# One subtraction (kt_l) moved from GpSimd to VectorE in a gated-linear-attention and channel-mix layer

## The chip, the cores and the metric

The kernel runs on all 8 cores of one Trainium2 chip. Each core works alone on its own slice of the tokens. The metric is the device time in microseconds (us) of the slowest core. The engines of a core are called here PE (TensorE), DVE (VectorE), ACT (ScalarE), POOL (GpSimd) and SP (SyncE, which issues all DMAs).

## The reference

The layer has two halves, each added back to its input through a layer norm. All sizes are fixed: 2 sequences of 16384 tokens, width 1024, 8 heads of 128.

```python
# first half: gated linear attention on x = layernorm(input)
q = silu(x @ Wq.T)
f = sigmoid(x @ Wk.T)
log_f = log_sigmoid(f)
k = 1.0 - f
v = x @ Wv.T
# per head, over time:  S = exp(g_t)[:, None] * S + k_t[:, None] * v_t[None, :];  o_t = q_t @ S
out = rmsnorm(gla_scan(q, k, v, log_f), norm_w) @ Wo.T
x = input + layernorm(out)
# second half: channel mix on layernorm(x), with the token before mixed in
xr = mu_r * x + (1 - mu_r) * x_prev;  xk = mu_k * x + (1 - mu_k) * x_prev
out = sigmoid(xr @ W_r.T) * (square(relu(xk @ W_k.T)) @ W_v.T)
x = x + layernorm(out)
```

## The kernel before, in words

Each core gets 4096 tokens and 256 warm-up tokens ahead of them, so 4352 tokens or 17 tiles of 256 (`TILE`). Data lies transposed: the 1024 features are 8 blocks of 128 partitions, the tokens run along the free dimension. Every float32 operand X of a matmul is split in two bfloat16 tensors, X_h = bf16(X) and X_l = bf16(X - X_h), and each product is made of three matmuls (h*h, h*l, l*h).

Phase A (attention) runs first over all tiles, then phase B (output projection and channel mix), with its own weights. The change lies in phase A alone.

Phase A treats a tile as two chunks of 128 tokens (`cc` 0 and 1). The loop has 18 rounds for 17 tiles: in round `it` it prepares the projections of tile p = it and works through the attention of tile q = it - 1. The order in which the parts of a round are written is: `a_bc(p)`, `a_prep(2q)`, `a_prep(2q+1)`, `a_vproj(2q)`, `a_gla(2q)`, `a_vproj(2q+1)`, `a_ln(p)`, `a_wk(p)`, `a_gla(2q+1)`, `a_wq(p)`, `a_stats(p+1)`. Each engine executes its own instructions in exactly this order; between engines there are only counting semaphores, one per engine (V for DVE, S for ACT, G for POOL, T for PE), and an instruction waits at the head of its queue until the counts it names are reached.

`a_prep` builds the operands of one chunk. Its instructions, in order:

- DVE L329: 8 running sums (one per head) of the log gate, `b_sb`. The first waits for the 8 exponentials of the chunk before (`ebx_done`), which read the old `b_sb`.
- ACT L333: `ebq` = exp(b + 44). ACT L336: `ebk` = exp(-b - 44).
- DVE L339: `qt_scr` = q * ebq. DVE L343: `qt_h`, the bfloat16 copy. DVE L345: `qt_l` = qt_scr - qt_h.
- POOL L349: `ebk` = k * ebk. ACT L353: `kt_h`, the bfloat16 copy. POOL L356: `kt_l` = ebk - kt_h. This last one is what the change moves.
- ACT L361: 8 exponentials (one per head) into `ebq`. POOL L367: `ebq` = k * ebq. ACT L370: `kx_h`. POOL L373: `kx_l`.

`a_vproj` has 48 matmuls of 512 columns on PE (L400) and then four DVE instructions that take the two PSUM banks out as `vt_h` (L408, L410) and `vt_l` (L412, L415). `a_gla` has 24 matmuls kt x qt into two PSUM banks (L446, these read `kt_h` and `kt_l`), their masking and splitting on DVE (L457, L460, L462, once per bank), 24 matmuls of the cross-chunk part (L479, which overwrite the same banks and so wait for L462), its splitting on DVE (L491, L494), and the output matmuls (L514, L531), which ACT takes out of PSUM (L547, L552). `a_ln` has four DVE instructions on 128 x 2048, `a_wk` and `a_wq` have 192 matmuls each (L250), `a_stats` has the row sums for the layer norm (L231, L235) and small DVE and ACT work on one partition.

`kt_h`, `kt_l`, `qt_h`, `qt_l` have two buffers (`par`), so both chunks of a tile are prepared before the first is used. `ebk` and `ebq` have one.

Of the kernel before, what the change touches and what calls it, by code (L numbers as in the profile page):

```python
# [24 lines left out]
class Bld:  # L25
# [12 lines left out]
    def op(self, eng, fn, wait=(), inc=(), nop=False):  # L38
        wmax = {}
        for s, v in wait:  # L40
            if v > 0:
                wmax[s] = max(v, wmax.get(s, 0))
        waits = tuple((self.sem[s], v) for s, v in wmax.items())
        ev = None
        incs = []
        for s, k in inc:
            self.cnt[s] += k
            incs.append((self.sem[s], k))
            ev = (s, self.cnt[s])

        def closure(e, fn=fn, waits=waits, incs=tuple(incs), nop=nop):
            for sem, v in waits:
                e.wait_ge(sem, v)
            if nop:
                e.engine_nop()
            ins = fn(e)
            for sem, k in incs:
                ins.then_inc(sem, k)

        self.q[eng].append(closure)  # L60
        return ev
# [27 lines left out]
    def ev(self, s):  # L89
        return (s, self.cnt[s])  # L90


def build_program(tok, warm, debug=False):
# [31 lines left out]
    op, ev, C = bld.op, bld.ev, bld.cnt  # L125
# [30 lines left out]
    for dst, src in ((mask4, mask4v), (onesc, onescv), (onesr, onesrv),  # L156
                     (nw, nwv), (mur, murv), (muk, mukv)):
        op("sync", lambda e, dst=dst, src=src: e.dma_start(out=dst[:], in_=src),
           inc=[("LW", 16)])
# [111 lines left out]
    ebk = ctxA.enter_context(nc.sbuf_tensor("ebk", [128, H, CH], F32))  # L271
    qt_h = ctxA.enter_context(nc.sbuf_tensor("qt_h", [128, 2, H, CH], BF16))
    qt_l = ctxA.enter_context(nc.sbuf_tensor("qt_l", [128, 2, H, CH], BF16))
    kt_h = ctxA.enter_context(nc.sbuf_tensor("kt_h", [128, 2, H, CH], BF16))
    kt_l = ctxA.enter_context(nc.sbuf_tensor("kt_l", [128, 2, H, CH], BF16))
# [44 lines left out]
    def a_prep(gc):  # L320
        q, cc = gc // 2, gc % 2
        tsl = slice(cc * CH, (cc + 1) * CH)
        par = gc % 2
        tpar = gc % 3
        fpar = q % 2
        aq = at[q]
        for h in range(H):
            wv = [aq["ev_g"], ("V", C["V"]), st["ebx_done"]] if h == 0 else ()
            op("vector", lambda e, h=h, tsl=tsl: e.tensor_tensor_scan(  # L329
                b_sb[:, h, :], g_sb[:, h, tsl], g_sb[:, h, tsl], 0.0, ALU.add, ALU.bypass),  # L330
               wait=wv, inc=[("V", 1)], nop=True)
        ev_b = ev("V")
        ev_ebq = op("scalar", lambda e: e.activation(out=ebq[:], in_=b_sb[:], func=AF.Exp,  # L333
                                                     bias=b_p44[:, 0:1]),
                    wait=[ev_b, st["ebq_free"], ("S", C["S"])], inc=[("S", 1)])
        ev_ebk = op("scalar", lambda e: e.activation(out=ebk[:], in_=b_sb[:], func=AF.Exp,  # L336
                                                     bias=b_m44[:, 0:1], scale=-1.0),
                    wait=[ev_b, st["ebk_free"]], inc=[("S", 1)])
        op("vector", lambda e, tsl=tsl, fpar=fpar: e.tensor_tensor(  # L339
            qt_scr[:], fq_sb[:, fpar, :, tsl], ebq[:], ALU.mult),  # L340
           wait=[aq["ev_q"], ev_ebq, ("V", C["V"])], inc=[("V", 1)])
        ev_qtmul = ev("V")
        op("vector", lambda e, par=par: e.tensor_copy(qt_h[:, par], qt_scr[:]),  # L343
           wait=[st["qt_free"][par], ("V", C["V"])], inc=[("V", 1)])
        op("vector", lambda e, par=par: e.tensor_tensor(qt_l[:, par], qt_scr[:],  # L345
                                                        qt_h[:, par], ALU.subtract),
           wait=[("V", C["V"])], inc=[("V", 1)])
        ev_qt = ev("V")
        op("gpsimd", lambda e, tsl=tsl: e.tensor_tensor(ebk[:], k_sb[:, :, tsl], ebk[:],  # L349
                                                        ALU.mult),  # L350
           wait=[aq["ev_k"], ev_ebk, ("G", C["G"])], inc=[("G", 1)])
        ev_ktmul = ev("G")
        ev_kth = op("scalar", lambda e, par=par: e.activation(  # L353
            out=kt_h[:, par], in_=ebk[:], func=AF.Copy),
            wait=[st["kt_free"][par], ev_ktmul, ("S", C["S"])], inc=[("S", 1)])
        op("gpsimd", lambda e, par=par: e.tensor_tensor(kt_l[:, par], ebk[:], kt_h[:, par],  # L356
                                                        ALU.subtract),
           wait=[ev_kth, ("G", C["G"])], inc=[("G", 1)])
        ev_kt = ev("G")
        for h in range(H):  # L360
            op("scalar", lambda e, h=h: e.activation(  # L361
                out=ebq[:, h, :], in_=b_sb[:, h, :], func=AF.Exp, scale=-1.0,
                bias=b_sb[:, h, CH - 1:CH]),
               wait=[ev_qtmul, ev_b, ("S", C["S"])], inc=[("S", 1)])
        ev_ebx = ev("S")
        st["ebx_done"] = ev_ebx
        ev_kxmul = op("gpsimd", lambda e, tsl=tsl: e.tensor_tensor(  # L367
            ebq[:], k_sb[:, :, tsl], ebq[:], ALU.mult),
           wait=[ev_ebx, ("G", C["G"])], inc=[("G", 1)])
        ev_kxh = op("scalar", lambda e, tpar=tpar: e.activation(  # L370
            out=kx_h[:, tpar], in_=ebq[:], func=AF.Copy),
            wait=[st["kx_free"][tpar], ev_kxmul, ("S", C["S"])], inc=[("S", 1)])
        op("gpsimd", lambda e, tpar=tpar: e.tensor_tensor(kx_l[:, tpar], ebq[:],  # L373
                                                          kx_h[:, tpar], ALU.subtract),
           wait=[ev_kxh, ("G", C["G"])], inc=[("G", 1)])
        ev_kx = ev("G")
        st["kx_ready"][tpar] = ev_kx
        st["ebq_free"] = ev_kx
        st["ebk_free"] = ev_kt
        st["k_free"] = ("G", C["G"])  # L380
        if cc == 1:
            st["fq_free"][fpar] = ev_qtmul
            st["g_free"] = ev_b
        prep.setdefault(gc, {}).update(
            dict(ev_b=ev_b, ev_qt=ev_qt, ev_kt=ev_kt, par=par, tpar=tpar))
# [271 lines left out]
    for it in range(nt + 1):  # L657
        p, q = it, it - 1
        if p < nt:
            a_bc(p)  # L660
        if q >= 0:
            a_prep(2 * q)
            a_prep(2 * q + 1)
            a_vproj(2 * q)
            a_gla(2 * q)
            a_vproj(2 * q + 1)
        if p < nt:
            a_ln(p)
            a_wk(p)
        if q >= 0:  # L670
            a_gla(2 * q + 1)
        if p < nt:
            a_wq(p)
            if p + 1 < nt:
                a_stats(p + 1)
        bld.flush()
# [355 lines left out]
```

How the kernel before makes its waits and increments, by code:

```python
        def closure(e, fn=fn, waits=waits, incs=tuple(incs), nop=nop):  # L51
            for sem, v in waits:
                e.wait_ge(sem, v)
            if nop:
                e.engine_nop()
            ins = fn(e)
            for sem, k in incs:
                ins.then_inc(sem, k)
# [11 lines left out]
        def closure(e, waits=waits):  # L70
            for sem, v in waits:
                e.wait_ge(sem, v)
```

## Time and profile before

| | |
|---|---|
| median of 2 runs | 5805.86 us (5741.52 and 5870.21) |
| profiled execution, its own time | 5803.8 us |
| profiled execution, span of the slowest core (5) | 5801.9 us |
| profiled execution, fastest core (2) | 5730.5 us |
| phase A, rounds with attention | about 245 to 2650 us of the span, 17 rounds |
| phase B, tiles | from about 2868 us to the end |

The profile is of one execution, and its page is of core 5, the slowest. "Busy" is the time in which an engine executes; "idle before" an instruction is put down to what released it, as inferred from the semaphores. The "granted clock" is the share of full speed that TensorE was granted in a stretch. All eight cores do the same work on different tokens.

### The profile page before, as it was taken

To read this page: it belongs to the slowest core of one execution; us is meant where nothing else is said; L and a number is where in the kernel's file an instruction comes from. 1 tells how busy PE (TensorE), PEld (TensorE's weight loads), DVE (VectorE), ACT (ScalarE), POOL (GpSimd) and SP (SyncE) were. 2 spreads that over 40 slices of the span, in tenths; PEclk is the share of its full clock that TensorE was granted. 3 is DMA by queue.
4 is the path that set the end of the run, shared out by engine and by line. 5 is a ranking of instruction groups with operands and counts; after the bars stand their busy time and mean duration, and the time that the engine had idled before them with its cause. 6 is when DMAs were issued, how large, how long until landed. Compare 5 with 4: busy or idle time off the path is not lost.

```text
span 5801.9 us, 65888 instructions; the slowest of 8 cores (5730.5 to 5801.9 us)
## 1 busy us (share of the span) xinstructions
PE 3535.2 (61%) x26608; PEld 2641.5 (46%) x26608; DVE 1951.1 (34%) x1944; ACT 1059.1 (18%) x1597; POOL 530.6 (9%) x239
## 2 busy tenths in 40 slices
PE   0566666666666666661166556766565667665676
PEld 0344444444444444441155444555444455544454
DVE  1333333333333333342133333232333332233323
ACT  0222222222222222230011111111111111111010
POOL 1111111111111111111200000000000000000000
PEclk9877778777777777775588778888887877777777
DMA  2000000000000000002200000000000000000000
GB/s 81 26 15 14 15 15 15 14 15 15 15 15 15 15 15 15 15 8 62 76 15 15 22 22 22 22 1 23 22 22 22 22 22 1 22 22 22 22 8 8
DMA packets 114735, 121.83 MB, mean 21 GB/s; under 512 B 3683, under 2 KB 107270, under 8 KB 114438
## 3 DMA queue, kind: packets, MB, share of 16 engines
q1 hardware_dynamic: 114438, 117.63, 6.6%
q8 instruction: 215, 3.52, 0.3%
q14 instruction: 82, 0.67, 0.0%
HBM read 83.00 MB, written 34.62 MB: 20 GB/s over the span
## 4 chain that ended last, share of the span: by engine, by line
PE 53%; DVE 26%; ACT 7%; DMA 5%; issue 5%; POOL 3%; DVEq 1%; ACTq 0%; SPq 0%; POOLq 0%
PE p_pj L250 39%; PE p_st L231 4%; PE p_pj L400 3%; DVE b_sb L329 3%; PE p_O L514 1%; PE p_O L531 1%; DVE r_a L207 1%; DMA outT<-x_sb 1%; ACT ebq L361 1%; DVE p_A L457 1%; DVE qt_h L343 1%; PE p_A L479 1%; DVE A_l L462 1%; DVE A_h L460 1%; DMA oB<-o_scr 1%
## 5 line engine op out<-in xcount | busy, mean ns | idle before, releaser
L250 PE MATMUL p_pj<-o_pair,woh 128*128 128x256 bf16 x2176 | 423.5, 302 | 538.1 <-POOL o_pair L763 306.1
L250 PEld LDWEIGHTS p_pj<-o_pair,woh 128*128 128x128 bf16 x2176 | 232.0, 108 | 599.5 <-issue 553.4
L231 PE MATMUL p_st<-x_sb,onesc 128*1 128x256 f32 x544 | 182.3, 509 | 475.1 <-ACT oB L897 270.6
L250 PE MATMUL p_pj<-ln_h,wkh 128*128 128x256 bf16 x1088 | 308.3, 283 | 199.6 <-DVE ln_l L613 199.6
L250 PE MATMUL p_pj<-xk_h,wv2h 128*128 128x256 bf16 x1088 | 318.6, 293 | 118.9 <-DVE xk_l L821 118.9
L231 PEld LDWEIGHTS p_st<-x_sb,onesc 128*1 128x1 f32 x544 | 55.3, 105 | 601.1 <-issue 577.6
L250 PE MATMUL p_pj<-o_pair,wol 128*128 128x256 bf16 x1088 | 327.0, 301 | 0.0
L250 PE MATMUL p_pj<-xr_h,wrh 128*128 128x256 bf16 x1088 | 306.5, 282 | 24.8 <-DVE xk_l L938 24.8
L250 PE MATMUL p_pj<-xk_l,wv2h 128*128 128x256 bf16 x1088 | 318.4, 293 | 0.0
L250 PE MATMUL p_pj<-xk_h,wv2l 128*128 128x256 bf16 x1088 | 317.5, 292 | 0.0
L250 PE MATMUL p_pj<-ln_h,wqh 128*128 128x256 bf16 x1088 | 310.7, 286 | 2.5 <-ACT fq_sb L648 2.5
L250 PE MATMUL p_pj<-ln_h,wql 128*128 128x256 bf16 x1088 | 309.9, 285 | 0.0
L250 PE MATMUL p_pj<-ln_l,wqh 128*128 128x256 bf16 x1088 | 309.6, 285 | 0.0
L250 PE MATMUL p_pj<-ln_l,wkh 128*128 128x256 bf16 x1088 | 308.5, 284 | 0.0
L250 PE MATMUL p_pj<-ln_h,wkl 128*128 128x256 bf16 x1088 | 307.3, 282 | 0.0
L250 PE MATMUL p_pj<-xr_h,wrl 128*128 128x256 bf16 x1088 | 306.4, 282 | 0.0
L250 PE MATMUL p_pj<-xr_l,wrh 128*128 128x256 bf16 x1088 | 306.3, 282 | 0.0
L250 PE MATMUL p_pj<-xk_h,wk2h 128*128 128x256 bf16 x1088 | 303.2, 279 | 0.0
L250 PE MATMUL p_pj<-xk_l,wk2h 128*128 128x256 bf16 x1088 | 303.2, 279 | 0.0
L250 PE MATMUL p_pj<-xk_h,wk2l 128*128 128x256 bf16 x1088 | 303.2, 279 | 0.0
L479 PE MATMUL p_A<-qt_h,kx_h 128*128 128x128 bf16 x264 | 71.4, 280 | 370.9 <-DVE A_l L462 370.9
L761 POOL CAST o_pair<-oB 128x2048 bf16<-128x2048 f32 x17 | 32.1, 1889 | 2524.4 <-DMA oB<-o_scr 2524.4
(176 smaller groups left out, 7956.9 us busy)
## 6 DMA issues: line engine op xcount, KB each, us to landing
x_sb<-xT SPq DMA_DIRECT2D x17, 1024.0 KB, 5.4
o_scr<-o_stage SPq DMA_DIRECT2D x68, 256.0 KB, 2.3
oB<-o_scr SPq DMA_DIRECT2D x17, 1024.0 KB, 5.4
xB<-xT SPq DMA_DIRECT2D x17, 1024.0 KB, 5.5
outT<-x_sb SPq DMA_DIRECT2D x16, 1024.0 KB, 4.5
wstage<-wkT SPq DMA_DIRECT2D x8, 512.0 KB
wstage<-wqT SPq DMA_DIRECT2D x8, 512.0 KB
wstage<-wvT SPq DMA_DIRECT2D x8, 512.0 KB
```

The costliest lines, as they stand in the source:

```text
L207: op("vector", lambda e: e.reciprocal(r_a[:], r_t0[:]), wait=[("S", C["S"])], inc=[("V", 1)], nop=True)
L231: op("tensor", lambda e, ci=ci: e.matmul(p_st[0:1, 0:TILE], onesc[:], x_ap[:, ci, :], start=(ci == 0), stop=(ci == NCH - 1)), wait=wv if c ...
L250: e.matmul(bank[:, 0:TILE], wop[:, ci, dj * 128:(dj + 1) * 128], xop[:, ci, :], start=first, stop=last),
L329: op("vector", lambda e, h=h, tsl=tsl: e.tensor_tensor_scan(b_sb[:, h, :], g_sb[:, h, tsl], g_sb[:, h, tsl], 0.0, ALU.add, ALU.bypass), wa ...
L343: op("vector", lambda e, par=par: e.tensor_copy(qt_h[:, par], qt_scr[:]), wait=[st["qt_free"][par], ("V", C["V"])], inc=[("V", 1)])
L361: op("scalar", lambda e, h=h: e.activation(out=ebq[:, h, :], in_=b_sb[:, h, :], func=AF.Exp, scale=-1.0, bias=b_sb[:, h, CH - 1:CH]), wait ...
L400: e.matmul(bank[:], lnop[:, ci, tsl], wop[:, ci, half * 512:(half + 1) * 512], start=first, stop=last),
L457: op("vector", lambda e, bank=bank: e.tensor_tensor(bank[:], bank[:], mask4[:], ALU.mult), wait=[ev_Amm[g4], ("V", C["V"])], inc=[("V", 1)])
L460: op("vector", lambda e, bank=bank, Ah=Ah: e.tensor_copy(Ah[:], bank[:]), wait=[("V", C["V"])], inc=[("V", 1)])
L462: op("vector", lambda e, bank=bank, Ah=Ah, Al=Al: e.tensor_tensor(Al[:], bank[:], Ah[:], ALU.subtract), wait=[("V", C["V"])], inc=[("V", 1)])
L479: e.matmul(bank[:, (h - 4 * g4) * 128:(h - 4 * g4 + 1) * 128], kop[:, xpar, h, :], qop[:, h, :], start=first, stop=last),
L514: e.matmul(obank[:, (h - 4 * g4) * 128:(h - 4 * g4 + 1) * 128], vop[:, par, h, :], aop[:, (h - 4 * g4) * 128:(h - 4 * g4 + 1) * 128], star ...
```

## The change

One instruction of `a_prep` moves from POOL's queue to DVE's: the subtraction `kt_l` = ebk - kt_h. Its place in the text of the kernel stays the same, so on DVE it stands behind `qt_l` (L345) and ahead of the next `a_prep`'s first running sum (for the first chunk of a tile) or ahead of `a_vproj`'s `vt_h` (for the second). It waits for ACT's `kt_h`, for POOL's product `ebk` and for DVE's own instruction before it, and counts up V instead of G. What waited for it (PE's L446 and, through `ebk_free`, ACT's L336 of the next chunk) now waits for V.

```diff
         ev_kth = op("scalar", lambda e, par=par: e.activation(
             out=kt_h[:, par], in_=ebk[:], func=AF.Copy),
             wait=[st["kt_free"][par], ev_ktmul, ("S", C["S"])], inc=[("S", 1)])
-        op("gpsimd", lambda e, par=par: e.tensor_tensor(kt_l[:, par], ebk[:], kt_h[:, par],
+        op("vector", lambda e, par=par: e.tensor_tensor(kt_l[:, par], ebk[:], kt_h[:, par],
                                                         ALU.subtract),
-           wait=[ev_kth, ("G", C["G"])], inc=[("G", 1)])
-        ev_kt = ev("G")
+           wait=[ev_kth, ev_ktmul, ("V", C["V"])], inc=[("V", 1)])
+        ev_kt = ev("V")
```

## Rows read from the trace of the kernel before

**Rows 1.** The page, part 1: busy time, share of the span, instructions.
```profile
PE 3535.2 (61%) x26608; PEld 2641.5 (46%) x26608; DVE 1951.1 (34%) x1944; ACT 1059.1 (18%) x1597; POOL 530.6 (9%) x239
```

**Rows 2.** Waits of all engines: us in total, times, longest.
```profile
PE p_A L479 <- DVE A_l L462: 370.9, 66, 19.4
...
POOL ebq L367 <- ACT ebq L361: 51.9, 34, 1.8
```

**Rows 3.** Timeline of DVE, one round: start, us, instruction, [idle before <-releaser].
```profile
1118.16 2.84 DVE L329 TENSOR_TENSOR_SCAN b_sb<-g_sb 128x128 f32<-128x128 f32 x8
...
1127.89 1.23 DVE L345 TENSOR_TENSOR qt_l<-qt_scr,qt_h 128x1024 bf16<-128x1024 f32 x1
1132.87 6.76 DVE L329 TENSOR_TENSOR_SCAN b_sb<-g_sb 128x128 f32<-128x128 f32 x8 [3.76 <-ACT ebq L361]
...
1142.83 2.29 DVE L343 CAST qt_h<-qt_scr 128x1024 bf16<-128x1024 f32 x1 [0.46 <-DVE qt_scr L339]
1145.23 1.23 DVE L345 TENSOR_TENSOR qt_l<-qt_scr,qt_h 128x1024 bf16<-128x1024 f32 x1
1146.56 0.69 DVE L408 CAST vt_h<-p_pj 128x512 bf16<-128x512 f32 x1
...
1153.73 0.69 DVE L462 TENSOR_TENSOR A_l<-p_A,A_h 128x512 bf16<-128x512 f32 x1
```

**Rows 4.** Timeline of PE, the same round.
```profile
1133.48 0.22 PE L446 MATMUL p_A<-qt_h,kt_l 128*128 128x128 bf16 x1
...
1152.18 0.26 PE L479 MATMUL p_A<-qt_h,kx_h 128*128 128x128 bf16 x1 [18.48 <-DVE A_l L462]
```

**Rows 5.** Timeline of ACT, the same round.
```profile
1127.66 1.06 ACT L353 ACTIVATE kt_h<-ebk 128x1024 bf16<-128x1024 f32 x1 [2.99 <-POOL ebk L349]
...
1144.72 1.06 ACT L353 ACTIVATE kt_h<-ebk 128x1024 bf16<-128x1024 f32 x1 [2.70 <-POOL ebk L349]
1145.87 3.86 ACT L361 ACTIVATE ebq<-b_sb 128x128 f32<-128x128 f32 x8
```

**Rows 6.** Timeline of POOL, the same round.
```profile
1128.92 2.18 POOL L356 TENSOR_TENSOR kt_l<-ebk,kt_h 128x1024 bf16<-128x1024 f32 x1 [1.68 <-ACT kt_h L353]
1132.87 2.56 POOL L367 TENSOR_TENSOR ebq<-k_sb,ebq 128x1024 f32<-128x1024 f32 x1 [1.77 <-ACT ebq L361]
...
1142.16 2.41 POOL L349 TENSOR_TENSOR ebk<-k_sb,ebk 128x1024 f32<-128x1024 f32 x1 [3.16 <-ACT ebk L336]
1145.98 2.45 POOL L356 TENSOR_TENSOR kt_l<-ebk,kt_h 128x1024 bf16<-128x1024 f32 x1 [1.41 <-ACT kt_h L353]
1149.93 2.34 POOL L367 TENSOR_TENSOR ebq<-k_sb,ebq 128x1024 f32<-128x1024 f32 x1 [1.50 <-ACT ebq L361]
```

**Rows 7.** Groups by line and shape, whole span: busy us, mean ns, idle before.
```profile
L356 POOL TENSOR_TENSOR kt_l<-ebk,kt_h 128x1024 bf16<-128x1024 f32 x34 | 82.7, 2431 | 48.7 <-ACT kt_h L353 45.3 <-ACT ebq L361 3.4
...
L345 DVE TENSOR_TENSOR qt_l<-qt_scr,qt_h 128x1024 bf16<-128x1024 f32 x34 | 41.7, 1225 | 3.5
...
L408 DVE CAST vt_h<-p_pj 128x512 bf16<-128x512 f32 x34 | 23.5, 692 | 148.1 <-PE p_pj L400 146.3
```

**Rows 8.** Busy us (instructions) by window, PE to POOL, granted clock, DMA share, GB/s.
```profile
1152.20:1157.60 5.40, 4.44 (x41) 4.20 (x42) 4.71 (x7) 1.06 (x1) 2.19 (x2) 0.50 0.00 0
1157.80:1161.00 3.20, 1.31 (x23) 1.05 (x21) 0.00 (x0) 1.23 (x2) 0.00 (x0) 1.00 0.27 80
```

**Rows 9.** Timeline of DVE: the first qt_scr of two rounds that follow each other.
```profile
977.05 1.23 DVE L339 TENSOR_TENSOR qt_scr<-fq_sb,ebq 128x1024 f32<-128x1024 f32 x1 [2.80 <-ACT ebq L333]
...
1123.80 1.22 DVE L339 TENSOR_TENSOR qt_scr<-fq_sb,ebq 128x1024 f32<-128x1024 f32 x1 [2.80 <-ACT ebq L333]
```

**Rows 10.** Cores: us from first to last instruction, mean granted TensorE clock.
```profile
core 2: 5730.5 us, clock 0.801
...
core 5: 5801.9 us, clock 0.788
```

## The prediction, made before the changed kernel was run

> **What bounds the kernel now.** I read the page first. PE is busy for 61% of the span, DVE for 34%, POOL for 9% [rows 1]: no engine is full, so the time is a chain that passes from engine to engine, and what an instruction costs depends on whether it lies on it. The waits say where PE stands still in the part that the change touches. PE's longest-lasting wait there is for DVE's `A_l` (L462): 370.9 us in 66 times, up to 19.4 us each [rows 2]. Then I laid the timelines of one round side by side, from 1118 to 1160 us. PE has finished the 48 matmuls of `a_vproj(2q)` and the 24 of L446 by 1133.7 us and idles for 18.48 us until DVE has worked through the preparation of both chunks, the four `vt` instructions and the first masking [rows 4]. So from about 1118 to 1154 us the round is set by the preparation, in which DVE, ACT and POOL hand work to each other.
>
> Inside it there are two kinds of stretch, and the reader should see both in rows 3. Between `qt_l` of the first chunk (ends 1129.12) and the running sums of the second (start 1132.87) DVE is idle for 3.76 us, because the sums wait for ACT's eight exponentials. Behind `qt_l` of the second chunk (ends 1146.46) there is no idle time at all: `vt_h` starts at 1146.56, 0.10 later, and DVE runs on without a stop to the last `A_l` at 1154.42. This holds in all 17 rounds: of the 34 L408 the idle time is 148.1 us, and 146.3 of that is waiting for PE's L400 [rows 7]; that is 8.6 us on each of the 17 in the second half of a round, which leaves 0.1 for each of those that follow `a_prep`.
>
> **The change, part by part.**
>
> *Taken from POOL.* 34 instructions of 2.43 us mean [rows 7]. What stood behind each is the product L367. It did not start late because of `kt_l`: in both chunks it was released by ACT's L361, after 1.77 and 1.50 us of POOL idleness [rows 6], and over the span it waited 34 times for L361 [rows 2]. Worth 0. Without this cover (if L361 were done at once) the gain would be the 2.4 us that POOL is freed.
>
> *`kt_l` ready earlier.* In the first chunk POOL ended it at 1131.10 and DVE will end it at about 1130.45. Its reader is PE's L446, which stands behind the 48 matmuls of `a_vproj(2q)` and is through with `kt_l` at 1133.7 [rows 4], while the next thing on the chain, DVE's L457, comes only at 1149.74, since DVE itself is late. In the second chunk POOL ended it at 1148.43 [rows 6]; its reader is on PE's queue behind the whole of `a_gla(2q)`, which cannot go on before 1152.18 [rows 4]. ACT's L336 of the next chunk, which now waits for V, is released by the running sums, 9 us later. Worth 0 in all three.
>
> *Added to DVE, first chunk.* The nearest row is `qt_l` (L345): the same operation, the same 128 x 1024, one float32 and one bfloat16 input from SBUF, bfloat16 out, 1.225 us in the mean of 34 [rows 7], and I take that. Its operand is there: `kt_h` ends at 1128.72 [rows 5], 0.40 us before `qt_l` does. So `kt_l` runs from 1129.22 to 1130.45, inside the 3.76 us in which DVE waits for ACT. 2.4 us of slack remain. Cost 0; without that cover it would be 1.33.
>
> *Added to DVE, second chunk.* `kt_h` ends at 1145.78 [rows 5], 0.68 us before `qt_l`, so the instruction does not wait, and runs from 1146.56 to 1147.79. Queued behind it on DVE are `vt_h` and everything up to `A_l`, none of which had idle time, and PE's L479 waits for the last. Start to start the cost is what L345 to L408 is now: 1146.56 - 1145.23 = 1.33 us (1.23 and 0.10 between two instructions). From there the whole rest of the round is late by it: the output matmuls, ACT's evictions, the 48 matmuls of `a_vproj(2q+1)`, `a_ln`, the 192 matmuls of `a_wk`. I find no wait in it that ends on something fixed.
>
> *Bounds of that duration.* Below: the running sums on DVE show what POOL does to it. Eight of them take 2.84 us while POOL rests and 6.76 us while L367 and L373 run beside them [rows 3], and the cast `qt_h` ends 0.55 us after POOL's L349 does (1145.12 against 1144.57) [rows 3, 6]. So a DVE instruction can be held until a POOL instruction is over. The nearest such row gives the upper end for `kt_l`: 2.4 us more. In the slot in question POOL has nothing: the `kt_l` that was there is gone, and L367 comes at 1149.93 [rows 6], 2.1 us after `kt_l` is done. I take 1.33. The lower end is 1.33 too, as nothing shows a faster form.
>
> The Trainium skill (page "SBUF — State Buffer", section "Who interferes with whom") says that a VectorE instruction with two SBUF inputs contends with a GpSimd instruction that reads SBUF. That rule speaks against this change, since `kt_l` is of that kind. In these rows the sums fit it; by it, too, a POOL instruction would have to overlap, and in neither slot does one.
>
> *The sum.* 17 rounds x 1.33 = 22.6 us, on the profiled execution's own 5803.8 us: 5826.4 us. The median of the runs shown is 5805.9, 2 us off that, so the base is a fair one. Phase B is untouched.
>
> **What the clock may make of it.** PE's granted clock has two levels here. Behind the long idle time PE starts L479 at 1152.18, and until 1157.6 the window reads 0.50 (1.2 GHz), from 1157.8 to 1161 it reads 1.00 (2.4 GHz) [rows 8]. If the rise stays where it is when PE's work comes 1.33 us later, that much less of the work is done at half speed, and half of the delay is given back there; the same can happen at each later rise of the round. If on the other hand the delay makes a rise come too late, a stretch such as the 3.2 us at 1.00 is passed at half speed, for 1.6 us more. That the first of these has some force is seen in how steady the rounds are: from 977.05 to 1123.80 it is 146.75 us [rows 9]. So the cost per round lies between 0 and 1.33 + 1.6 = 2.93 us. I see no ground to prefer a side and leave the term at 1.33, near the middle (1.47).
>
> **Rivals.**
>
> A. *The delay is absorbed.* Each rise of the clock gives half back until nothing is left by the end of the round. For it: the steadiness above. Against it: it needs several rises per round that all stay put. Time: 5804.
>
> B. *A rise comes too late in every round.* 17 x 2.93 = 49.8: 5854. For it: the full-speed stretch is short, so it is easily missed. Against it: what is missed here may be gained at the next one.
>
> C. *POOL holds DVE.* `kt_l` of the second chunk, or what it pushes, meets a POOL instruction that reads SBUF and waits it out: 17 x (1.33 + 2.4) = 63.4: 5867. It decides if DVE's `kt_l` starts less than 1.23 us before L367, that is, if `qt_l` ended about 2.1 us later than it does. Against it: in all I looked at POOL is idle there, and L408 to L462 read one side from PSUM and are 0.69 us long beside a running POOL (L462 at 1153.73, with L373 running). A change of over 2% upward would need 6.8 us per round; nothing in the rows has that size.
>
> D. *It is faster.* The DVE instruction is 1.21 us shorter than POOL's (2.43 - 1.225), and if the hand-over from `ebk` to L446 set the pace, 34 x 1.21 = 41 us would be gained: 5763. Against it: PE is idle for 18 us after it has read `kt_l` [rows 4]. The Trainium skill (page "GPSIMD Engine Reference", section "8. Key points") calls VectorE structurally about twice as fast for elementwise work. The trace agrees, with 1.225 against 2.431 us, but an instruction off the chain does not shorten it.
>
> **How the numbers follow.** The forecast, 1.33 us per round with the clock neutral, has 0.50, A 0.22, B 0.14, C 0.07, D 0.07. The predicted time is 5826. All five lie within 63 us of the base. What spreads a measurement more is the clock: core 2 and core 5 do the same work in 5730.5 and 5801.9 us at clocks 0.801 and 0.788 [rows 10], and the two runs shown are 64 us to either side of their median. Around 5804 to 5826, and with most but not all of that scatter, I take 5755 to 5885. About 2% (116 us) is what a measurement of this kernel can tell from no change; no case reaches it by itself, so it takes scatter on top: faster 0.02, same 0.93, slower 0.05.
>
> **What would show it right or wrong.** In the timeline of the changed kernel: DVE's `kt_l` of the first chunk lies in the idle time before the running sums, whose start does not move against `qt_l` (5.0 us start to start); that of the second chunk is 1.23 us long with `vt_h` 1.33 us later behind `qt_l` (2.65 us start to start); PE's wait for `A_l` grows from 18.5 to 19.8 us per round. The round's length then tells forecast, A and B apart: 148.1, 146.75 or up to 149.7. A `kt_l` of over 2 us on DVE would show C; a shorter idle time of PE before L479 would show D. POOL's L367 must still be released by L361.

## The result

| | before | changed |
|---|---|---|
| median of all runs | 5757.18 us (16 runs) | 5773.78 us (17 runs) |
| lowest run | 5740.9 us | 5767.05 us |
| ratio, changed to before | | 1.0031, 95% interval 1.0020 to 1.0043 |
| profiled execution, spans of the 8 cores | 5730.5 to 5801.9 us | 5754.3 to 5763.5 us |

The changed kernel is slower by 0.31%, which is 18 us (12 to 25). The forecast had the sign and nearly the size of the step (22.6 us). Its absolute number, 5826, is 52 us above the median, and most of that is the base, not the step. Some executions of either kernel have one half of the chip at a lower clock and are longer; the ratios, and the times called undisturbed below, leave them out.

The page of the changed kernel, part 1 (busy time of each engine, share of the span, instructions), to be held against [rows 1]:

```profile
PE 3462.2 (60%) x26574; PEld 2615.5 (45%) x26608; DVE 1999.8 (35%) x1978; ACT 1058.9 (18%) x1597; POOL 448.2 (8%) x205
```

POOL has 34 instructions and 82.4 us less, DVE 34 instructions and 48.7 us more. Both engines together work 34 us less, and the kernel takes 18 us more.

The timeline of DVE in the changed kernel, in the round that answers to [rows 3] (start, us, instruction, idle before it and its releaser; core 2, the slowest):

```profile
1125.89 1.23 DVE L345 TENSOR_TENSOR qt_l<-qt_scr,qt_h 128x1024 bf16<-128x1024 f32 x1
1127.22 1.23 DVE L356 TENSOR_TENSOR kt_l<-ebk,kt_h 128x1024 bf16<-128x1024 f32 x1
1130.87 6.76 DVE L329 TENSOR_TENSOR_SCAN b_sb<-g_sb 128x128 f32<-128x128 f32 x8 [2.43 <-ACT ebq L361]
...
1143.23 1.23 DVE L345 TENSOR_TENSOR qt_l<-qt_scr,qt_h 128x1024 bf16<-128x1024 f32 x1
1144.56 1.23 DVE L356 TENSOR_TENSOR kt_l<-ebk,kt_h 128x1024 bf16<-128x1024 f32 x1
1145.89 0.69 DVE L408 CAST vt_h<-p_pj 128x512 bf16<-128x512 f32 x1
...
1153.06 0.69 DVE L462 TENSOR_TENSOR A_l<-p_A,A_h 128x512 bf16<-128x512 f32 x1
```

The same instruction stands twice in the round and has two prices. In the first place the idle time before the running sums shrinks from 3.76 to 2.43 us, and the sums start 4.98 us after `qt_l`, as before. In the second `vt_h` starts 2.66 us after `qt_l` instead of 1.33, and all up to `A_l` moves with it. PE shows it: on core 2 its long wait ahead of L479 is 19.0 to 19.8 us in the changed kernel's rounds, 19.03 in this one, where [rows 4] has 18.48 and the other rounds of the kernel before have 17.7 to 18.6. Over the span (waits of core 2: us in total, times, longest):

```profile
PE p_A L479 <- DVE A_l L462: 390.2, 66, 20.9
...
POOL ebq L367 <- ACT ebq L361: 183.0, 34, 5.6
```

The first line was 370.9 [rows 2]. In the second, POOL now stands idle for 5.4 us ahead of each L367, for the same releaser as before: POOL's relief bought nothing.

### The profile page after: what moved, and what is told of

It reads as the page before. It is cut to its first block, busy times and chain, and to the rows that moved or that the text cites. A ratio compares the mean times of both kernels' runs of the same rounds, so it can differ in the third digit from the quotient of the medians.

```text
span 5763.5 us, 65787 instructions; the slowest of 8 cores (5754.3 to 5763.5 us)
## 1 busy us (share of the span) xinstructions
PE 3462.2 (60%) x26574; PEld 2615.5 (45%) x26608; DVE 1999.8 (35%) x1978; ACT 1058.9 (18%) x1597; POOL 448.2 (8%) x205
## 4 chain that ended last, share of the span: by engine, by line
PE 52%; DVE 26%; ACT 7%; DMA 5%; issue 5%; POOL 3%; DVEq 1%; ACTq 0%; SPq 0%; POOLq 0%
PE p_pj L250 39%; PE p_st L231 4%; PE p_pj L400 4%; DVE b_sb L329 3%; PE p_O L514 1%; PE p_O L531 1%; DVE r_a L207 1%; DMA outT<-x_sb 1%; ACT ebq L361 1%; DVE p_A L457 1%; PE p_A L479 1%; DVE A_l L462 1%; DVE A_h L460 1%; POOL ebk L349 1%; ACT xsq_bf L552 1%
## 5 line engine op out<-in xcount | busy, mean ns | idle before, releaser
L231 PE MATMUL p_st<-x_sb,onesc 128*1 128x256 f32 x544 | 168.1, 478 | 469.0 <-ACT oB L897 269.6
L479 PE MATMUL p_A<-qt_h,kx_h 128*128 128x128 bf16 x264 | 71.5, 280 | 390.2 <-DVE A_l L462 390.2
L817 DVE TENSOR_TENSOR scr<-scr 128x2048 f32<-128x2048 f32 x17 | 39.0, 2292 | 634.9 <-ACT scr L810 634.9
```

What stands on the lines that cost most here:

```text
L231: op("tensor", lambda e, ci=ci: e.matmul(p_st[0:1, 0:TILE], onesc[:], x_ap[:, ci, :], start=(ci == 0), stop=(ci == NCH - 1)), wait=wv if c ...
L479: e.matmul(bank[:, (h - 4 * g4) * 128:(h - 4 * g4 + 1) * 128], kop[:, xpar, h, :], qop[:, h, :], start=first, stop=last),
```

## The experiments

The change touches only phase A, and the whole time also holds phase B, whose length differs between kernels too (last section). So beside each time I read the length of phase A, from the first to the last `qt_scr` (L339) of a core. For the kernel before and the changed one, core 3 (timeline of DVE, the first and the last L339; first pair before, second pair changed):

```profile
248.93 1.22 DVE L339 TENSOR_TENSOR qt_scr<-fq_sb,ebq 128x1024 f32<-128x1024 f32 x1 [2.75 <-ACT ebq L333]
...
2585.14 1.23 DVE L339 TENSOR_TENSOR qt_scr<-fq_sb,ebq 128x1024 f32<-128x1024 f32 x1 [1.52 <-ACT ebq L333]
```

```profile
248.51 1.23 DVE L339 TENSOR_TENSOR qt_scr<-fq_sb,ebq 128x1024 f32<-128x1024 f32 x1 [2.75 <-ACT ebq L333]
...
2606.71 1.23 DVE L339 TENSOR_TENSOR qt_scr<-fq_sb,ebq 128x1024 f32<-128x1024 f32 x1 [1.52 <-ACT ebq L333]
```

That is 2336.2 and 2358.2 us. The kernels that vary the place or the delay, with the delay per round that each puts into DVE's second place (instruction as measured, and 0.10 us between two), and the median of phase A over the cores:

| kernel | delay in the second place | phase A, median (range) | against before | whole time, ratio (interval) |
|---|---|---|---|---|
| before | 0 | 2338.4 (2336.2 to 2374.5) | | |
| changed | 1.33 | 2358.4 (2354.8 to 2361.9) | +20 | 1.0031 (1.0020 to 1.0043) |
| e1_first | 0 | 2343.5 (2339.7 to 2343.7) | +5 | 1.0024 (0.9972 to 1.0076) |
| e2_second | 1.33 | 2357.1 (2353.2 to 2360.5) | +19 | 1.0055 (1.0022 to 1.0088) |
| e3_late | 0 | 2340.0 (2336.1 to 2343.6) | +2 | 0.9992 (0.9950 to 1.0033) |
| v079_vth_twice | 0.79 | 2346.9 (2343.2 to 2348.5) | +8.5 | |
| d185_ktl_and_quarter | 1.85 | 2374.3 and 2377.3 (cores 6 and 7) | +37 | |
| d212_ktl_and_half | 2.12 | 2352.1 (2350.3 to 2356.9, cores 4 to 7) | +14 | |
| d079_half_qtl | 2.52 | 2354.2 (2351.5 to 2358.6) | +16 | |
| d266_ktl_twice | 2.66 | 2372.3 (2371.8 to 2395.7) | +34 | 1.0104 (1.0051 to 1.0158) |
| d133_qtl_twice | 3.06 | 2394.4 (2391.1 to 2394.9) | +56 | 1.0066 (1.0026 to 1.0105) |

The median of the kernel before holds two cores (6 and 7, 2363.3 and 2374.5 us) whose first rounds had a lower clock. The other six lie at 2336.2 to 2340.1 us with a median of 2336.4, and held against that every difference in the table is 2 us larger. Each kernel's phase A is read from one execution.

### Which of the two places costs

`e1_first` and `e2_second` each make half of the change:

```diff
+        if cc == 0:      # e2_second: if cc == 1
+            op("vector", ... kt_l[:, par], ebk[:], kt_h[:, par], ALU.subtract ...)
+        else:
+            op("gpsimd", ... the same ...)
```

> kt_l is on DVE only for the first chunk of a tile, on POOL for the second, as before. Theory (second chunk only): DVE's kt_l lies in the 3.76 us in which DVE waits for ACT's exponentials, so the time is that of the kernel before, 0 us, with PE's wait for A_l at 18.5 us per round. Rival (any further DVE instruction in the preparation costs its length): 17 x 1.33 = 22.6 us more, or half of the changed kernel's 18 us, 9 us, if both places share the cost.

> kt_l is on DVE only for the second chunk of a tile. Theory: the whole of the changed kernel's cost, 18 us (ratio 1.003), with PE's wait for A_l 1.33 us longer per round. Rival (both places share the cost): about 9 us.

PE's wait for `A_l` (waits of core 4, `e1_first` and then `e2_second`):

```profile
PE p_A L485 <- DVE A_l L468: 371.1, 66, 19.8
```

```profile
PE p_A L485 <- DVE A_l L468: 390.0, 66, 20.4
```

The first place leaves the wait where it was, the second adds the changed kernel's 19 us. In phase A it is +5 against +19. The 5 us are there in this execution (six of its eight cores lie above 2343 us, over the 2340.1 of the kernel before), but nearly all of them come in the first rounds. The ten rounds from the sixth to the sixteenth first-chunk `qt_scr` of core 3 take 1467.7 us before, 1468.1 in `e1_first`, 1478.3 in `e2_second` and 1481.3 in the changed kernel. The whole times are less clear: the interval of `e1_first` holds 0 and also the changed kernel's step, and that of `e2_second` holds the changed kernel's. In both, phase B is some 20 us longer than in the changed one (last section). That the cost sits in the second place is shown by the waits and by phase A.

### The place or the work

`e3_late` keeps all 34 subtractions on DVE but issues that of the second chunk behind `a_gla(2q)`:

```diff
             a_gla(2 * q)
+            issue_ktl()      # kt_l of chunk 2q+1, on DVE
             a_vproj(2 * q + 1)
```

> kt_l is on DVE for both chunks, but that of the second chunk is issued behind the whole of the first chunk's a_gla, where DVE waits 8.6 us for the matmuls of a_vproj. The same 34 instructions run on DVE as in the changed kernel. Theory (the place in DVE's queue costs, not the work): 0 us against the kernel before. Rival (the work or the longer hand-over of ebk costs): 18 us as in the changed kernel.

DVE of core 3 in this kernel:

```profile
1145.89 1.23 DVE L345 TENSOR_TENSOR qt_l<-qt_scr,qt_h 128x1024 bf16<-128x1024 f32 x1
1147.22 0.69 DVE L414 CAST vt_h<-p_pj 128x512 bf16<-128x512 f32 x1
...
1168.21 0.94 DVE L585 RECIPROCAL r_rms<-r_rms 1x128 f32<-1x128 f32 x1 [1.96 <-ACT r_rms L581]
1169.26 1.22 DVE L357 TENSOR_TENSOR kt_l<-ebk,kt_h 128x1024 bf16<-128x1024 f32 x1
```

`vt_h` is back at 1.33 us behind `qt_l`, `kt_l` comes 22 us later and no instruction waits for it. Phase A is +2 us, and the ten rounds of core 3 take 1462.7 us, less than before. The ratio, 0.9992 (0.9950 to 1.0033), agrees, though its interval reaches up to 19 us more, so it is phase A that tells the rivals apart. The work on DVE costs nothing here; its place in the queue does.

### The same delay with POOL's instruction still there

`d133_qtl_twice` is the kernel before with `qt_l` of the second chunk computed twice, `d079_half_qtl` the same with half of its elements:

```diff
+        if cc == 1:
+            op("vector", ... qt_l[:, par], qt_scr[:], qt_h[:, par], ALU.subtract ...)
+            # d079_half_qtl: [..., 0:4] of each, 512 elements
```

> The kernel before, kt_l on POOL, with DVE's qt_l of the second chunk computed twice: the same 1.33 us on DVE at the same place, and nothing moved. Theory (occupancy of DVE at this place): as the changed kernel, 18 us, 1.003. Rival (freeing POOL or the shorter kt_l gives part of it back in the changed kernel): more than that, 22.6 us or above.

> The kernel before with half of the second chunk's qt_l (512 of 1024 elements) computed twice: 0.69 us and 0.10 between two instructions, 0.79 us later per round. Theory L (the delay adds up): 17 x 0.79 = 13.4 us. Theory C (the granted clock's rises stay where they are and absorb a small delay until one is missed): 0 us, with the round's length still 146.77 us.

I had taken both for clean doses of 1.33 and 0.79 us. They are not. DVE and POOL of core 6 of `d133_qtl_twice`:

```profile
1163.73 1.23 DVE L345 TENSOR_TENSOR qt_l<-qt_scr,qt_h 128x1024 bf16<-128x1024 f32 x1
1165.06 2.96 DVE L349 TENSOR_TENSOR qt_l<-qt_scr,qt_h 128x1024 bf16<-128x1024 f32 x1
```

```profile
1164.48 2.46 POOL L360 TENSOR_TENSOR kt_l<-ebk,kt_h 128x1024 bf16<-128x1024 f32 x1 [1.41 <-ACT kt_h L357]
```

The first `qt_l` takes 1.23 us, the repeated one 2.96, and it ends at 1168.02, 1.08 us after POOL's `kt_l` (1166.94). A DVE instruction of 1.23 us that cannot start until about the end of POOL's fits that. Half of it is held just as long (groups by line of core 4 of `d079_half_qtl`; busy, mean ns of one):

```profile
L349 DVE TENSOR_TENSOR qt_l<-qt_scr,qt_h 128x512 bf16<-128x512 f32 x17 | 41.2, 2425 | 1.8
```

2425 ns, where 512 elements of the same form took 692 without POOL beside them (in `d212_ktl_and_half`). Held by 1.73 us each, the whole and the half differ only by their own lengths. So the real delays are 3.06 and 2.52 us per round, and phase A is 56 and 16 us longer. The cost of `d133_qtl_twice` went the rival's way, but the reason is neither of the two I had written down: POOL's `kt_l` is not merely work, it holds DVE. This is rival C of the prediction, met where POOL's `kt_l` is kept: the changed kernel pays only 1.33 us because the instruction that would have held DVE is the one that was moved. The Trainium skill (page "SBUF — State Buffer", section "Who interferes with whom") has VectorE instructions with two SBUF inputs contend with GpSimd instructions that read SBUF; these rows agree.

### Does a delay add up, or does the clock take it back?

Four kernels vary the delay. `v079_vth_twice` is the kernel before with the first `vt_h` of the first chunk computed twice; the other three are the changed kernel with a quarter, a half or the whole of the second chunk's `kt_l` computed again:

```diff
+        if cc == 0:      # v079_vth_twice, behind the first vt_h
+            op("vector", ... tensor_copy(vt_h[:, par, 0:4, :], p_pj[0][:]) ...)
+        if cc == 1:      # the other three, behind kt_l: n = 2, 4 or 8 heads of 128
+            op("vector", ... kt_l[:, par, 0:n], ebk[:, 0:n], kt_h[:, par, 0:n], ALU.subtract ...)
```

> The kernel before with the first vt_h of the first chunk computed twice. It reads PSUM, so a running POOL instruction should not hold it (0.69 us, where the repeated half of qt_l, with both inputs in SBUF, took 2.42 us beside POOL's kt_l). DVE's chain is 0.79 us later per round. Theory L (delays add up): phase A 13.4 us longer. Theory C (a small delay is absorbed by the clock's rises, which do not move with it): phase A 0 to 3 us longer, most rounds still 146.8 us.

> The changed kernel with half of the second chunk's kt_l computed again: 1.33 + 0.79 = 2.12 us later per round than before. Theory L: 17 x 2.12 = 36 us over the kernel before. Theory C, as it follows from replaying one round of PE's instructions of the kernel before with its own clock steps: the delay is absorbed nearly whole, 0 to 5 us over the kernel before and so faster than the changed kernel, although more work is done; the round's length returns to 146.8 us.

> The changed kernel with the second chunk's kt_l computed twice: 2.66 us later per round than before. Theory L: 17 x 2.66 = 45 us over the kernel before. Theory C by the same replay: the round jumps to 148.5 or 150.2 us, so 27 to 58 us, not on a line through the smaller delays.

> The changed kernel with a quarter of the second chunk's kt_l (256 elements) computed again: 1.33 + 0.42 + 0.10 = 1.85 us later per round than before, which lies between the changed kernel (1.33 us, phase A 20 us longer) and the one with half of kt_l again (2.12 us, phase A 14 us longer). Theory L: 17 x 1.85 = 31 us. Theory C, by the replay of one round with its own clock steps: one rise is missed in every round, rounds of 150.2 us, phase A 45 to 58 us longer, so more than with 2.12 us.

In these texts L is "delays add up" and C is "the clock's rises stay where they are, so that a small delay is absorbed until one of them is missed". The replay is a calculation of mine that is not printed here: it takes the durations of PE's instructions in one round of the kernel before, puts the delay in, and computes anew which of them run at the lower clock. It is a model; what counts is what the runs say.

The smallest dose first. Ten rounds of core 3, from the sixth to the sixteenth first-chunk `qt_scr`, before and then in `v079_vth_twice`:

```profile
969.81 1.23 DVE L339 TENSOR_TENSOR qt_scr<-fq_sb,ebq 128x1024 f32<-128x1024 f32 x1 [2.80 <-ACT ebq L333]
...
2437.54 1.23 DVE L339 TENSOR_TENSOR qt_scr<-fq_sb,ebq 128x1024 f32<-128x1024 f32 x1 [2.80 <-ACT ebq L333]
```

```profile
982.00 1.23 DVE L339 TENSOR_TENSOR qt_scr<-fq_sb,ebq 128x1024 f32<-128x1024 f32 x1 [2.80 <-ACT ebq L333]
...
2449.70 1.23 DVE L339 TENSOR_TENSOR qt_scr<-fq_sb,ebq 128x1024 f32<-128x1024 f32 x1 [2.80 <-ACT ebq L333]
```

1467.73 and 1467.70 us. PE's long wait for `A_l` is longer in these rounds, by 0.79 us in most (19.0 against 18.2), and over the span it is 382.7 us against 370.4. Yet ten rounds together are not longer at all. The 8.5 us in the table, where C had said 0 to 3, came in the rounds before these. The repeated `vt_h` itself took 0.69 us: with its input in PSUM nothing held it.

For the larger doses, phase A of core 4 of `d212_ktl_and_half` (delay 2.12 us) and of core 3 of `d266_ktl_twice` (2.66 us):

```profile
250.13 1.23 DVE L339 TENSOR_TENSOR qt_scr<-fq_sb,ebq 128x1024 f32<-128x1024 f32 x1 [2.75 <-ACT ebq L333]
...
2600.51 1.23 DVE L339 TENSOR_TENSOR qt_scr<-fq_sb,ebq 128x1024 f32<-128x1024 f32 x1 [1.52 <-ACT ebq L333]
```

```profile
249.11 1.23 DVE L339 TENSOR_TENSOR qt_scr<-fq_sb,ebq 128x1024 f32<-128x1024 f32 x1 [2.75 <-ACT ebq L333]
...
2621.21 1.22 DVE L339 TENSOR_TENSOR qt_scr<-fq_sb,ebq 128x1024 f32<-128x1024 f32 x1 [1.52 <-ACT ebq L333]
```

2350.4 and 2372.1 us. `d212_ktl_and_half` does more on DVE than the changed kernel and its phase A is shorter than any of the changed kernel's eight (2354.8 to 2361.9). The replay had said 0 to 5 us; it is 14, so the size was missed, but by L it should have been 34 (16 delays lie in phase A as it is measured here). `d266_ktl_twice` is 34 us longer, inside the replay's 27 to 58.

`d185_ktl_and_quarter` lies between those two in dose (1.85 us). In its profiled execution the clock of most cores fell within phase A. Cores 6 and 7 kept it to the end of phase A and give the table's figure; core 0 kept it for the first 13 rounds. These are its first and fourteenth first-chunk `qt_scr`, and the same two of core 0 before:

```profile
251.07 1.23 DVE L339 TENSOR_TENSOR qt_scr<-fq_sb,ebq 128x1024 f32<-128x1024 f32 x1 [2.75 <-ACT ebq L333]
...
2184.20 1.23 DVE L339 TENSOR_TENSOR qt_scr<-fq_sb,ebq 128x1024 f32<-128x1024 f32 x1 [2.80 <-ACT ebq L333]
```

```profile
246.79 1.23 DVE L339 TENSOR_TENSOR qt_scr<-fq_sb,ebq 128x1024 f32<-128x1024 f32 x1 [2.75 <-ACT ebq L333]
...
2146.07 1.23 DVE L339 TENSOR_TENSOR qt_scr<-fq_sb,ebq 128x1024 f32<-128x1024 f32 x1 [2.80 <-ACT ebq L333]
```

1933.13 against 1899.28: 33.9 us over 13 rounds, 2.6 us per round, more than the 1.85 put in; nine of the 13 rounds lasted 150.1 to 150.5 us. Core 4 of `d212_ktl_and_half` lost 10.7 us over the same 13 rounds, 0.8 per round. The one undisturbed time of `d185_ktl_and_quarter` is 5812 us, that of `d212_ktl_and_half` 5775. That is one run each, but it points the same way. The replay's 45 to 58 us for phase A was too high: cores 6 and 7 are 36 to 39 us above the table's median before.

So L falls: 0.79, 1.33, 1.85, 2.12, 2.52, 2.66 and 3.06 us put in give, per round, 0.5, 1.3, 2.3, 0.9, 1.0, 2.1 and 3.5 us of phase A (the table's figures over 16). From 1.85 to 2.12 the delay grows by 0.27 us and the cost falls by 1.4.

What differs between a short and a long round is PE's clock. One round of core 3 before, then a short and a long one of core 3 of the changed kernel (window, length, busy us and instructions of PE, PEld, DVE, ACT, POOL; granted clock; DMA share; GB/s):

```profile
969.81:1116.55 146.74, 95.51 (x718) 69.17 (x717) 53.13 (x63) 42.11 (x62) 20.54 (x9) 0.79 0.05 15
```

```profile
1419.94:1566.72 146.78, 94.55 (x718) 68.96 (x717) 55.59 (x65) 42.12 (x62) 15.90 (x7) 0.79 0.05 15
1863.64:2013.75 150.11, 97.56 (x717) 70.26 (x716) 55.59 (x65) 42.12 (x62) 15.91 (x7) 0.77 0.05 15
```

In the two rounds of the changed kernel DVE, ACT and POOL are busy equally long. The long one is longer by 3.33 us, PE needs 3.01 us more for the same matmuls, and its granted clock is 0.77 instead of 0.79. My estimate from these two figures is that PE's clock stands at the lower level (0.50) for about 7 us more, which costs half of that. The short round keeps the length of before although DVE's chain is 1.33 us longer, and PE is busy for 1.0 us less in it: more of its work falls at the full clock. So both halves of theory C are in the trace. Which rounds become long is not shown by any row. The replay said before the run that 2.12 us would cost less than 1.33, and later, with that measured, that 1.85 would cost more than either; both came true, with two of its three sizes wrong.

### What the waits pointed to: another order

PE's 18.5 us wait is there because DVE prepares the second chunk before it takes out and masks the first. Three kernels change that order. In `o1_order` `a_prep(2q+1)` is issued behind `a_gla(2q)`; in `o2_between` it is issued inside `a_gla(2q)`, ahead of the row statistics (L571); `o3_between_dve` is `o2_between` with the change under study.

```diff
             a_prep(2 * q)
-            a_prep(2 * q + 1)
             a_vproj(2 * q)
-            a_gla(2 * q)
+            a_gla(2 * q, between=lambda q=q: a_prep(2 * q + 1))
             a_vproj(2 * q + 1)
```

> The kernel before, but a_prep(2q+1) is issued behind a_gla(2q) instead of ahead of a_vproj(2q); kt_l stays on POOL. If the preparation of the second chunk is what keeps DVE from the first chunk's masking, PE's 18.5 us idle time ahead of L479 shrinks to about 4 us and the preparation falls beside the matmuls of a_vproj(2q+1), with some of it left over because it starts only once the first chunk's row statistics are done: 5 to 10 us per round gained, 85 to 170 us, ratio 0.97 to 0.985. Rival: the preparation is as long there and only changes places with the idle time: 0 us.

> As the kernel with the other order, but a_prep(2q+1) is issued ahead of the first chunk's row statistics (L571 on), so that DVE can start its running sums right behind Ax_l; kt_l on POOL. Expected: 2 to 6 us per round better than the order alone, 0.96 to 0.98 of the kernel before. Rival: ACT's order or POOL's products set the pace there, and it is equal to the order alone.

> The same order with kt_l on DVE, as in the changed kernel. In this order the second chunk's kt_l stands ahead of vt_h of the second chunk. If DVE still waits for PE's L400 there, it costs 0 us against the same order with kt_l on POOL; if the preparation ends after the matmuls, it costs 1.33 us per round or 23 us, less where POOL's queue had become what sets the pace.

| kernel | undisturbed times | ratio to before (interval) | phase A, median |
|---|---|---|---|
| before (same chip) | 5747 to 5781 us | | 2338 |
| o1_order | 5568 us | | 2191 |
| o2_between | 5574, 5576, 5582 us | 0.968 (0.963 to 0.973) | 2185 |
| o3_between_dve | 5574, 5577 us | 0.968 (0.961 to 0.975) | 2190 |

The reordered kernels beat the kernel before by 3.2% on the same chip. `o1_order` has one undisturbed time, 5568 us, some 190 below, where 85 to 170 was expected; its phase A is 147 us shorter. PE's wait, of core 4 of `o2_between`:

```profile
PE p_A L479 <- DVE A_l L462: 152.0, 66, 8.2
```

370.9 us have become 152.0. `o2_between` is no better than `o1_order`, against what I expected. Its DVE shows why (core 4):

```profile
1087.00 1.23 DVE L345 TENSOR_TENSOR qt_l<-qt_scr,qt_h 128x1024 bf16<-128x1024 f32 x1
1088.33 0.28 DVE L573 TENSOR_SCALAR r_rms<-p_st 1x128 f32<-1x128 f32 x1
1097.15 0.94 DVE L581 RECIPROCAL r_rms<-r_rms 1x128 f32<-1x128 f32 x1 [8.54 <-ACT r_rms L577]
1098.20 0.69 DVE L408 CAST vt_h<-p_pj 128x512 bf16<-128x512 f32 x1
```

The preparation is done early, but then the reciprocal waits 8.54 us for a square root (L577), which on ACT's queue stands behind the second chunk's exponentials and copies (its L370 ends at 1095.25, the square root at 1097.02), and `vt_h` is queued behind the reciprocal. The head of a queue has moved, not gone. In this order the change under study costs 5 us of phase A (2190 against 2185), a quarter of its cost before, and no difference in the whole time.

## Why the prediction was right or wrong

**What bounds the round.** Right. PE's wait for `A_l` grew by 19 us over the span (370.9 [rows 2] to 390.2), and the reordering that removes most of the wait gains 3.2%.

**POOL's relief is worth 0.** Right, by the releaser of L367, which is ACT's L361 in both kernels.

**First place: 0, inside 3.76 us.** Right in the trace (idle 3.76 to 2.43) and in `e1_first`'s wait. Phase A of `e1_first` is 5 us longer in the median, nearly all of it in the first rounds: the ten rounds after them are 0.4 us longer together. What lengthened the first ones is open.

**Second place: 1.33 us per round.** Right in length and place (2.66 us from `qt_l` to `vt_h`), and `e3_late` shows that it is the place.

**No POOL instruction in the slot.** Right, and more important than it was made: with POOL's `kt_l` left in, the same DVE instruction took 2.96 us.

**The clock, 0 to 2.93 us per round, taken at 1.33.** Both mechanisms are real, so A and B are not rivals to the forecast but take turns. Of core 3's 16 distances from round to round in the changed kernel, the 14 between the first and the last lie between 146.7 and 150.1 us. Seven are within 0.3 us of the 146.75 of [rows 9]: there the whole delay is given back, as A has it. Two are 150.0 and 150.1, up to 3.3 us longer, so B's 2.93 us and its longest round of 149.7 were too small. No term of 1.33 us in each round is in this. The step that I sized at 22.6 us measured 17.8 in the whole time (12 to 25) and 20 in phase A, where 16 of the 17 delays lie and 21.3 was due. That the mean of such rounds lies near 1.33 is luck: with 1.85 and 2.12 us put in, the same reckoning misses by +7 and -20 us of phase A.

**The base.** This step failed. "The median of the runs shown is 5805.9, 2 us off that, so the base is a fair one" rested on two runs 129 us apart. With 16 runs the median of before is 5757.2. Eleven of them lie between 5740.9 and 5770.0 and five between 5870 and 5965; the two shown were one of each kind, and their median lies where none of the 16 does. The forecast thus stood 69 us above the measured kernel before, where the change was worth 17 to 18. The profiled execution is 47 us above that median, and that is most of the 52 us by which 5826 is too high. It could be read in the trace. The windows 5000 to 5700 us of cores 3 and 5 of the kernel before (busy us and instructions of PE, PEld, DVE, ACT, POOL; granted clock; DMA share; GB/s):

```profile
5000.00:5700.00 700.00, 454.48 (x3621) 359.57 (x3619) 234.91 (x188) 79.29 (x134) 17.87 (x6) 0.83 0.05 16
```

```profile
5000.00:5700.00 700.00, 460.48 (x3270) 343.63 (x3268) 230.76 (x188) 78.91 (x126) 17.88 (x6) 0.75 0.05 16
```

Core 5, whose span I took as the base, had a clock of 0.75 there against 0.83, and its last tiles of phase B took 177 to 181 us against 167. Its phase A was like the others' (2340.1 us). The slowest of the cores 0 to 3, which have 0.81 to 0.83 in that window, had a span of 5751.2 us; with 22.6 and the 1.9 that the execution's time lies above its span that is 5775.7, against 5773.8 measured. Part of that closeness is luck: this base is 4 us below the median of before and the step 5 us too large. I had noted the difference between cores [rows 10] and put it in the range, where it belonged in the base.

**The rivals.** C is a real mechanism that this change happens to avoid: `kt_l` took 1.23 us on DVE in both places. D fell as argued: PE's idle time before L479 grew instead of shrinking. The change of sign that D stood for did not come.

## What to carry to other kernels

Ask of a moved instruction not which engine does it faster but what stands behind it in the queue that it joins, and whether that has idle time: here the same 1.23 us left the long wait alone at one place and lengthened it by all of itself at another, and an order of three calls was worth ten times the change. Before a base is taken from one execution, look whether the core that it comes from kept its clock. And a delay of a microsecond on a chain that stops and starts TensorE did not add up here. Over phase A it cost from 0.4 times its length (2.12 us put in) to 1.3 times (1.85), and in single stretches nothing; give such a term a range and not a value.

## What the runs showed of the hardware that I had not expected

A repeating round in which TensorE stops and starts can keep its length against small changes. In the kernel before, 11 of core 3's 16 rounds last 146.4 to 147.2 us; with 0.79 us more of waiting in each, ten rounds took the same time to 0.03 us. The changed kernel's rounds are of that length or up to 3.3 us longer, with a lower granted clock in the long ones.

Phase B has the same instructions in all these kernels, and its length, from the first `o_pair` to the end, still differs between them by more than the change is worth: medians of 2871 us (`d133_qtl_twice`), 2877 (changed), 2879 (`e3_late`), 2891 (`d266_ktl_twice`), 2899 (`e1_first`) and 2900 (`e2_second`), with all eight cores of a kernel within 16 us of each other. Its tiles last about 167.3 or about 170.4 us. Core 5 of `e1_first` in two tiles that follow each other (windows as above, from the cast that opens a tile, `o_pair`, to the next):

```profile
3438.21:3605.75 167.54, 108.50 (x853) 84.88 (x852) 57.62 (x47) 20.31 (x33) 5.95 (x3) 0.83 0.06 20
3605.75:3776.67 170.92, 111.74 (x855) 86.02 (x853) 57.61 (x47) 20.32 (x33) 5.96 (x3) 0.80 0.06 19
```

Again the other engines are busy equally long, and PE has the lower granted clock and 3.2 us more of busy time in the longer tile. The kernels with half of the change have more of the long ones. I did not find what sets how many there are; no change of mine touches phase B, so the layout of the program or what precedes the phase could do it, and no run here tells these apart. It stays open, and it is why the whole times of `e1_first` and `e2_second` lie some 20 us above what their phase A explains.
